# Small norm, gate and softmax operations of a cross-attention and mixture-of-experts kernel, moved from VectorE to other engines

## The chip, the cores and the metric

The kernel runs on one core of a Trainium2 chip. The time is that of one execution on the device, in microseconds (us). Engines: TensorE (PE in the profile), VectorE (DVE), ScalarE (ACT), GpSimd (POOL) and SyncE (SP), which here only issues DMAs.

## The reference

`x` is 8 x 1024 x 1024, `ctx` 8 x 64 x 1024 with a mask of its 64 rows, all float32. Cut to what matters:

```python
xn = layernorm(x)
scores = where(mask, xn @ ctx.T / sqrt(1024), -1e30)
x = x + where(any(mask), softmax(scores) @ ctx, 0)
xn = layernorm(x)
probs = softmax(xn @ router_w.T)                    # 8 experts
w_dense = the two largest of probs, divided by their sum, at their experts; 0 elsewhere
Ax = xn @ lora_A.T                                  # 8 experts x rank 16
x = x + xn @ weight.T + ((Ax * w_dense) @ lora_B) * 2.0
```

## The kernel before

The 8192 rows of x are 64 tiles of 128 rows (one row per partition); eight tiles make a batch element, which has its own ctx and mask. Every engine has its own list of instructions, written out by hand as `step(tile)` for each tile j of a batch; batches 1 to 6 are a hardware loop (`Fori`) on each engine. Semaphores order them: an engine waits with `wait_ge` until a count is reached, and everything behind that wait on the same engine waits too.

To keep float32 accuracy, each large product is done in three passes of split numbers (high and low part): `three` in `base` and `lora_second`, lines L1107 to L1109. The weights stay in SBUF. A `step` of TensorE for tile j has the base product of tile j (xn @ weight, lora_A and router together, in three groups of columns), at odd j the scores of a pair of tiles (L1134), the attention readout of tile j + 2 (L1179, L1180, needs `eT`), and the low-rank second product of tile j.

The path of one tile through the small operations:

- `softmax_scores` (VectorE) makes masked scores and their maximum; `softmax_exp` (ScalarE) exponentiates; `softmax_split` (VectorE) splits e and calls `softmax_sum`, which makes `e_scale` = `any_valid` / sum: a reciprocal (L888) and a product (L890). `e_transposes` turns 32 x 32 blocks, and `e_exchange` on SyncE (L417) moves the blocks in four copies to `e_raw`. ScalarE casts it to `eT` (L590), and the readout can go.
- `add_readout` (VectorE, L897) adds the readout times `e_scale` to x, `norm2_stats` (L903) takes the statistics of the new x, `hT_low` (L973) stands between, and `norm2_moments` makes the mean and variance (L908), `var_eps2` (L910) and `neg_mean2` (L911). Then VectorE goes on with `x2T_low` (L926), two subtractions of 128 x 512 that split the transposed xn of the tile before.
- GpSimd's `norm2` raises `var_eps2` to the power -1/2 (L494) and multiplies it with `neg_mean2` to `shift2` (L497). ScalarE's `norm2` makes `xn` from x with scale and bias (L609).
- `exchange` on SyncE (L381) moves xn to `xq` in four copies, and one step later VectorE turns blocks of it into `x2T` (`x2_transposes`, L919), ScalarE casts the high part (L615), VectorE makes the low part, and TensorE takes the base product.
- `router_top` waits for the router's columns of the base product and finds the two largest (L934 to L939). ScalarE's `gate_exp` makes `gate_num`, the exponential of their difference (L619). `router_gate` makes `gate_den` (L946), its reciprocal `gate_inv` (L949), `gate_b` and `w_dense` (L950, L953), and `h` (L965), which is turned, exchanged and split.

VectorE's order in `step(tile)`, where the change bears: `softmax_split` and `e_transposes` of tile j + 2, `router_top`, `router_gate` and `h_transposes` of tile j, `x2_transposes` of tile j + 1, at odd j `s_transposes` (sum of a pair of scores, L875), `add_readout` and `norm2_stats` of tile j + 2, `hT_low` of tile j, `norm2_moments` of tile j + 2, `x2T_low` of tile j + 1, `softmax_scores` of tile j + 3, then the sums of the output. In steps 3 to 6 the ctx of the next batch is centred and split in addition: `ctx_high` (ScalarE, L542) in step 5 and `ctx_low` (VectorE, L348) in step 6.

SyncE's order in `step(tile)` is `exchange` of xn of tile j + 2 (four copies, first a wait for it), then `e_exchange` of tile j + 3, the store, `h_exchange`, and loads.

For tiles 0 to 2 (and partly 3 and 4) the exchanges are done by TensorE's transposes instead, in orders of their own (`first_norm2` and others).

Of the kernel before, what the change touches and what calls it, by code (L numbers as in the profile page):

```python
# [23 lines left out]
def xattn_lora_moe_kernel(  # L24
# [10 lines left out]
    f32 = mybir.dt.float32  # L35
# [3 lines left out]
    ALU = mybir.AluOpType  # L39
# [69 lines left out]
    with stack:  # L109
# [61 lines left out]
        neg_mean2 = sb("neg_mean2", [P, 1])  # L171
        shift2 = sb("shift2", [P, 1])
# [96 lines left out]
        CONSTANTS = E + 4  # L269
# [37 lines left out]
        neg_mean2_done = sem("neg_mean2_done")  # L307
        shift2_done = sem("shift2_done")
# [164 lines left out]
        def _(pool):  # L473
# [18 lines left out]
            def norm2(tile):  # L492
                pool.wait_ge(ln2_step, count(tile, 4, 4))
# [38 lines left out]
        def _(act):  # L532
# [4 lines left out]
            def ctx_high(b):  # L537
# [4 lines left out]
                act.copy(ctx_hi[:, :], ctx_raw[:, 0:D]).then_inc(ctx_hi_done, 1)  # L542
# [34 lines left out]
            def softmax_exp(tile):  # L577
                act.wait_ge(softmax_step, count(tile, 5, 3))
# [13 lines left out]
            def first_softmax_exp(tile):  # L592
                act.wait_ge(softmax_step, count(tile, 5, 3))
# [166 lines left out]
        def _(dve):  # L760
# [68 lines left out]
            def softmax_scores(tile):  # L829
# [10 lines left out]
                dve.wait_ge(softmax_step, count(tile, 5, 1))  # L840
# [3 lines left out]
                dve.wait_ge(softmax_step, count(tile, 5, 2))  # L844
# [3 lines left out]
            def first_softmax_scores(tile):  # L848
# [542 lines left out]
```

## Time and profile before

| | us |
|---|---|
| median of 3 runs | 999.71 |
| lowest and highest | 997.89, 1001.46 |
| the profiled execution | 1000.15 |
| its span in the trace | 998.2 |
| TensorE matmul busy | 979.6 |
| VectorE busy | 868.6 |
| ScalarE busy | 476.0 |
| GpSimd busy | 144.0 |

The granted clock of TensorE is 1.00 of full speed over the whole span. Busy times are sums over one profiled execution. Matmuls overlap, so that TensorE's busy time doesn't say whether it stands before a given product; the starts of two neighbours do.

### The profile page before, as it was taken

Reading aid. Unit: us, or ns where it says so; the run is one execution under the profiler, and the core shown is the slowest. Engines: PE = TensorE matmul, PEld = TensorE weight load, DVE = VectorE, ACT = ScalarE, POOL = GpSimd, SP = SyncE. Lnnn points to the kernel's source line nnn. Section 1 sums busy time; section 2 is a strip of 40 time slices with the busy share of each in tenths; the row PEclk is TensorE's granted clock in tenths of the full one; section 3 lists DMA queues with packets and bytes.
Section 4 is the critical chain, followed back from the end, with each engine's and each line's share of the span. In section 5 each row is a group of like instructions: output and inputs, shape, how many; then the busy total and the mean of one; then the engine's idle time right before and its main releaser. Section 6 shows DMA issues by size and latency. Waiting matters only on the chain.

```text
span 998.2 us, 18389 instructions
## 1 busy us (share of the span) xinstructions
PE 979.6 (98%) x5849; PEld 950.2 (95%) x5849; DVE 868.6 (87%) x2230; ACT 476.0 (48%) x930; POOL 144.0 (14%) x278
## 2 busy tenths in 40 slices
PE   8999999999999999999999999999999999999998
PEld 7899999999999999999999999999999999999998
DVE  6988988889988899889989899888999889988874
ACT  7755544545444455445455445444454444454420
POOL 3311111111111111111111111111111111111100
PEclk9999999999999999999999999999999999999999
DMA  8555565555566555664555755556565566554432
GB/s 318 180 176 149 150 173 158 160 133 158 165 162 181 148 138 152 172 189 143 138 143 160 208 138 162 130 149 193 158 159 154 128 182 171 156 156 128 112 77 70
DMA packets 156095, 156.61 MB, mean 157 GB/s; under 512 B 93968, under 2 KB 128912, under 8 KB 156048
## 3 DMA queue, kind: packets, MB, share of 16 engines
q1 hardware_dynamic: 155184, 154.63, 56.2%
q10 hardware_dynamic: 864, 1.45, 0.4%
q8 instruction: 18, 0.29, 0.1%
q14 instruction: 29, 0.24, 0.1%
HBM read 78.74 MB, written 33.55 MB: 112 GB/s over the span
## 4 chain that ended last, share of the span: by engine, by line
PE 36%; DVE 22%; DMA 13%; SPq 10%; issue 8%; ACT 5%; POOL 5%; ACTq 0%; POOLq 0%; DVEq 0%
PE base_ps L1107 10%; PE base_ps L1109 10%; PE base_ps L1108 10%; DMA xq<-xn 10%; SPq L381 7%; DVE stats L903 5%; ACT xn L609 4%; DVE x2T L919 4%; DVE w_raw L897 3%; POOL rstd L494 3%; PE s_ps L1134 3%; SPq L417 2%; DMA w_raw<-w_raw 2%; DVE x_first L897 2%; PE ro_ps L1179 1%
## 5 line engine op out<-in xcount | busy, mean ns | idle before, releaser
L1107 PE MATMUL base_ps<-w_hi,xT_hi 128*128 128x392 f32 x1512 | 495.5, 328 | 0.0
L1109 PE MATMUL base_ps<-w_hi,xT_lo 128*128 128x392 f32 x1512 | 494.4, 327 | 0.0
L1108 PE MATMUL base_ps<-w_lo,xT_hi 128*128 128x392 f32 x1512 | 494.4, 327 | 0.0
L1107 PEld LDWEIGHTS base_ps<-w_hi,xT_hi 128*128 128x128 f32 x1512 | 285.9, 189 | 1.7
L1108 PEld LDWEIGHTS base_ps<-w_lo,xT_hi 128*128 128x128 f32 x1512 | 285.8, 189 | 1.6
L1109 PEld LDWEIGHTS base_ps<-w_hi,xT_lo 128*128 128x128 f32 x1512 | 285.8, 189 | 0.0
L919 DVE STREAM_TRANSPOSE x2T<-xq 128x512 f32<-128x512 f32 x122 | 167.2, 1465 | 27.7 <-DMA xq<-xn 27.6
L494 POOL TENSOR_TENSOR rstd<-var_eps,neg_half 128x1 f32<-128x1 f32 x64 | 61.4, 959 | 521.8 <-DVE var_eps L910 521.8
L615 ACT CAST xT_hi<-x2T 128x512 fp32r<-128x512 f32 x122 | 69.5, 616 | 100.9 <-DVE x2T L919 100.9
L590 ACT CAST eT<-w_raw 128x128 fp32r<-128x128 f32 x59 | 17.6, 298 | 166.6 <-DMA w_raw<-w_raw 166.5
L926 DVE TENSOR_TENSOR xT_lo<-x2T,xT_hi 128x512 fp32r<-128x512 f32 x122 | 78.2, 683 | 0.0
L609 ACT ACTIVATE xn<-w_raw,shift,rstd 128x1024 f32<-128x1024 f32 x32 | 39.7, 1241 | 78.6 <-POOL shift L497 78.6
L816 DVE TENSOR_TENSOR xT_parts<-xT_raw,xT_parts 128x1024 fp32r<-128x1024 f32 x62 | 73.4, 1185 | 0.0
L609 ACT ACTIVATE xn<-x_first,shift,rstd 128x1024 f32<-128x1024 f32 x29 | 36.0, 1241 | 71.5 <-POOL shift L497 71.5
L570 ACT CAST xT_parts<-xT_raw 128x1024 fp32r<-128x1024 f32 x64 | 63.8, 1043 | 0.1
L1107 PE MATMUL base_ps<-b_hi,hT_hi 128*128 128x384 f32 (+1 forms) x192 | 60.4, 315 | 1.4 <-DVE hT_lo L973 1.2
L1179 PE MATMUL ro_ps<-ctx_hi,eT 128*128 128x512 f32 x128 | 52.2, 407 | 7.6 <-ACT eT L590 7.0
L1108 PE MATMUL base_ps<-b_lo,hT_hi 128*128 128x384 f32 (+1 forms) x192 | 59.3, 309 | 0.0
L1109 PE MATMUL base_ps<-b_hi,hT_lo 128*128 128x384 f32 (+1 forms) x192 | 59.3, 309 | 0.0
L488 POOL TENSOR_TENSOR var_eps<-sum_sq,eps_sum 128x1 f32<-128x1 f32 x64 | 16.7, 261 | 276.9 <-ACT x2T L561 275.9
L1134 PE MATMUL s_ps<-xT_parts,ctxT 128*128 128x512 f32 x232 | 54.8, 379 | 0.0
L1180 PE MATMUL ro_ps<-ctx_lo,eT 128*128 128x512 f32 x128 | 48.5, 379 | 0.0
(131 smaller groups left out, 1274.2 us busy)
## 6 DMA issues: line engine op xcount, KB each, us to landing
xT_raw<-in_xT SPq DMA_DIRECT2D x62, 512.0 KB, 5.2
xq<-xn SPq DMA_DIRECT2D x244, 128.0 KB, 3.5
w_raw<-in_x SPq DMA_DIRECT2D x32, 512.0 KB, 3.4
out<-x_first SPq DMA_DIRECT2D x32, 512.0 KB, 2.7
out<-w_raw SPq DMA_DIRECT2D x31, 512.0 KB, 2.8
x_first<-in_x SPq DMA_DIRECT2D x30, 512.0 KB, 3.5
h<-w_raw SPq DMA_DIRECT2D x248, 16.0 KB, 2.1
w_raw<-w_raw SPq DMA_DIRECT2D x236, 16.0 KB, 2.6
```

Of the source, the lines that this page charges most:

```text
L381: sp.dma_start(xq[a * QP:(a + 1) * QP, :, :], xn[:, a * DQ:(a + 1) * DQ]).then_inc(xq_loaded, 16)
L494: pool.tensor_tensor(rstd2[:, :], var_eps2[:, :], neg_half[:, :], ALU.pow).then_inc(rstd2_done, 1)
L570: act.copy(xT_hi[:, i], xT_raw[:, k, i]).then_inc(xT_hi_done, 1)
L609: act.activation(xn[:, :], x(tile), ACT.Identity, bias=shift2[:, :], scale=rstd2[:, :]).then_inc(xn_done, 1)
L615: act.copy(chunks(xT2_hi[:, tile[1] % 2], i), chunks(x2T, i)).then_inc(x2T_hi_done, 1)
L816: dve.tensor_tensor(xT_lo[:, i], xT_raw[:, tile[1] // 2 % 2, i], xT_hi[:, i].bitcast(f32), ALU.subtract).then_inc(xT_split, 1)
L919: dve.transpose(out_[:, i * QS:(i + 1) * QS], xq[:, i * QS:(i + 1) * QS, :].rearrange("p g (c n) -> p g c n", n=QP)).then_inc(x2T_done, 1)
L926: dve.tensor_tensor(chunks(xT2_lo[:, k], i), chunks(x2T, i), chunks(xT2_hi[:, k], i).bitcast(f32), ALU.subtract).then_inc(x2T_split, 1)
L1107: pe.matmul(out_, a_hi, w_h, start=start, stop=False, skip_group_check=again)
L1108: pe.matmul(out_, a_hi, w_l, start=False, stop=False, skip_group_check=again)
L1109: return pe.matmul(out_, a_lo, w_h, start=False, stop=stop, skip_group_check=again)
L1134: mm = pe.matmul(s_ps[:, 0:2 * T2], ctxT[:, c, :], xT_parts[:, :, :, c, :].rearrange("p l t n -> p t n l"), start=(c == 0), stop=(c == C - 1))
```

## The change

Four operations on one column (128 x 1) leave VectorE in each tile:

- `var_eps2`, the variance plus epsilon, goes to GpSimd, ahead of its power;
- `neg_mean2` goes to ScalarE, as the first thing of its `norm2`, behind a wait for the mean;
- `gate_den` goes to ScalarE, behind `gate_num`; VectorE now makes `gate_b` ahead of the reciprocal;
- the product of the softmax's inverse sum with `any_valid` goes for tiles from batch 1 on (10 of 64 keep it); instead the ctx of those batches is multiplied with `any_valid` when it is split, in `ctx_high` and `ctx_low`.

Two constants more are set by GpSimd at the start, and the counts of the semaphores follow.

```diff
--- before.py
+++ after.py
@@ -266,7 +268,7 @@
-        CONSTANTS = E + 4
+        CONSTANTS = E + 6
...
@@ -345,8 +350,9 @@
         def ctx_low(engine, b):
             engine.wait_ge(ctx_hi_done, b + 1)
-            engine.tensor_tensor(ctx_lo[:, :], ctx_raw[:, 0:D], ctx_hi[:, :].bitcast(f32),
-                                 ALU.subtract).then_inc(ctx_split, 1)
+            engine.scalar_tensor_tensor(out=ctx_lo[:, :], in0=ctx_raw[:, 0:D], scalar=any_valid[:, :],
+                                        in1=ctx_hi[:, :].bitcast(f32), op0=ALU.mult,
+                                        op1=ALU.subtract).then_inc(ctx_split, 1)
...
@@ -478,6 +484,8 @@
+            pool.memset(eps_mean[:, :], EPS).then_inc(constants_ready, 1)
+            pool.memset(half_one[:, :], 1.0 / SCALING).then_inc(constants_ready, 1)
...
@@ -490,7 +498,9 @@
             def norm2(tile):
-                pool.wait_ge(ln2_step, count(tile, 4, 4))
+                pool.wait_ge(ln2_step, count(tile, 3, 3))
+                pool.tensor_tensor(var_eps2[:, :], mean_var2[:, 1:2], eps_mean[:, :], ALU.add).then_inc(var_eps2_done, 1)
+                pool.wait_ge(var_eps2_done, count(tile, 1, 1))
                 pool.tensor_tensor(rstd2[:, :], var_eps2[:, :], neg_half[:, :], ALU.pow).then_inc(rstd2_done, 1)
                 pool.wait_ge(neg_mean2_done, count(tile, 1, 1))
                 pool.wait_ge(rstd2_done, count(tile, 1, 1))
...
@@ -539,7 +549,11 @@
                 act.wait_ge(readout_done, count((b, 0), 2))
-                act.copy(ctx_hi[:, :], ctx_raw[:, 0:D]).then_inc(ctx_hi_done, 1)
+                if isinstance(b, int) and b == 0:
+                    act.copy(ctx_hi[:, :], ctx_raw[:, 0:D]).then_inc(ctx_hi_done, 1)
+                    return
+                act.wait_ge(mask_step, b * 3 + 3)
+                act.activation(ctx_hi[:, :], ctx_raw[:, 0:D], ACT.Identity, scale=any_valid[:, :]).then_inc(ctx_hi_done, 1)
...
@@ -603,7 +617,13 @@
+            def negative_mean2(tile):
+                act.wait_ge(ln2_step, count(tile, 3, 3))
+                act.wait_ge(shift2_done, count(tile, 1))
+                act.activation(neg_mean2[:, :], mean_var2[:, 0:1], ACT.Identity, scale=-1.0).then_inc(neg_mean2_done, 1)
+
             def norm2(tile):
+                negative_mean2(tile)
                 act.wait_ge(shift2_done, count(tile, 1, 1))
...
@@ -615,9 +635,12 @@
             def gate_exp(tile):
-                act.wait_ge(router_step, count(tile, 7, 1))
+                act.wait_ge(router_step, count(tile, 6, 1))
                 act.activation(gate_num[:, :], top8[:, 0:1], ACT.Exp, bias=top8[:, 1:2],
                                scale=-1.0).then_inc(gate_exp_done, 1)
+                act.wait_ge(gate_exp_done, count(tile, 1, 1))
+                act.activation(gate_den[:, :], gate_num[:, :], ACT.Identity, bias=half_one[:, :],
+                               scale=1.0 / SCALING).then_inc(gate_den_done, 1)
...
@@ -885,12 +909,16 @@
             def softmax_sum(tile):
-                dve.reciprocal(e_inv[:, :], e_sum[:, :]).then_inc(softmax_step, 1)
-                dve.wait_ge(softmax_step, count(tile, 5, 4))
+
+                if tile[0] > 0:
+                    dve.reciprocal(e_scale[:, :], e_sum[:, :]).then_inc(softmax_step, 1)
+                    return
+                dve.reciprocal(e_inv[:, :], e_sum[:, :]).then_inc(e_inv_done, 1)
+                dve.wait_ge(e_inv_done, count(tile, 1, 1))
                 dve.tensor_tensor(e_scale[:, :], e_inv[:, :], any_valid[:, :], ALU.mult).then_inc(softmax_step, 1)
...
@@ -903,12 +931,9 @@
             def norm2_moments(tile):
-                dve.wait_ge(ln2_step, count(tile, 4, 2))
+                dve.wait_ge(ln2_step, count(tile, 3, 2))
                 dve.sem_inc(waits_alone, 1)
                 dve.bn_aggr(mean_var2[:, :], stats2[:, :]).then_inc(ln2_step, 1)
-                dve.wait_ge(ln2_step, count(tile, 4, 3))
-                dve.tensor_scalar(var_eps2[:, :], mean_var2[:, 1:2], EPS, None, ALU.add).then_inc(ln2_step, 1)
-                dve.tensor_scalar(neg_mean2[:, :], mean_var2[:, 0:1], -1.0, None, ALU.mult).then_inc(neg_mean2_done, 1)
...
@@ -943,16 +968,15 @@
                 dve.wait_ge(gate_exp_done, count(tile, 1, 1))
-                dve.tensor_scalar(gate_den[:, :], gate_num[:, :], 1.0, 1.0 / SCALING, ALU.add, ALU.mult)\
-                   .then_inc(router_step, 1)
-                dve.wait_ge(router_step, count(tile, 7, 4))
-                dve.reciprocal(gate_inv[:, :], gate_den[:, :]).then_inc(router_step, 1)
+                dve.wait_ge(router_step, count(tile, 6, 3))
                 dve.tensor_scalar(gate_b[:, :], iota8[:, :], top2_at[:, 1:2], gate_num[:, :], ALU.is_equal, ALU.mult)\
                    .then_inc(router_step, 1)
-                dve.wait_ge(router_step, count(tile, 7, 6))
+                dve.wait_ge(gate_den_done, count(tile, 1, 1))
+                dve.reciprocal(gate_inv[:, :], gate_den[:, :]).then_inc(router_step, 1)
+                dve.wait_ge(router_step, count(tile, 6, 4))
                 dve.scalar_tensor_tensor(out=w_dense[:, :], in0=iota8[:, :], scalar=top2_at[:, 0:1], in1=gate_b[:, :],
                                          op0=ALU.is_equal, op1=ALU.add).then_inc(router_step, 1)
...
```

## Rows read from the trace of the kernel before

**Rows 1.** The page, part 1 (busy) and part 4 (the chain that ended last).

```profile
...
PE 979.6 (98%) x5849; PEld 950.2 (95%) x5849; DVE 868.6 (87%) x2230; ACT 476.0 (48%) x930; POOL 144.0 (14%) x278
...
PE base_ps L1107 10%; PE base_ps L1109 10%; PE base_ps L1108 10%; DMA xq<-xn 10%; SPq L381 7%; DVE stats L903 5%; ACT xn L609 4%; DVE x2T L919 4%; DVE w_raw L897 3%; POOL rstd L494 3%; PE s_ps L1134 3%; SPq L417 2%; DMA w_raw<-w_raw 2%; DVE x_first L897 2%; PE ro_ps L1179 1%
...
```

**Rows 2.** The waits: engine, line, releaser, us in total, times, longest.

```profile
...
DVE x2T L919 <- DMA xq<-xn: 27.6, 42, 2.8
...
PE ro_ps L1179 <- ACT eT L590: 7.0, 16, 1.4
...
```

**Rows 3.** The timeline of step 1 of batch 4: start, us, engine, line; in brackets idle before.

```profile
...
544.26 0.21 DVE L908 BATCH_NORM_AGGREGATE mean_var<-stats 128x2 f32<-128x12 f32 x1
...
544.50 0.15 DVE L910 TENSOR_SCALAR var_eps<-mean_var 128x1 f32<-128x1 f32 x1
...
544.58 0.14 DVE L911 TENSOR_SCALAR neg_mean<-mean_var 128x1 f32<-128x1 f32 x1
544.64 1.28 DVE L926 TENSOR_TENSOR xT_lo<-x2T,xT_hi 128x512 fp32r<-128x512 f32 x2
...
544.74 0.99 POOL L494 TENSOR_TENSOR rstd<-var_eps,neg_half 128x1 f32<-128x1 f32 x1 [9.37 <-DVE var_eps L910]
...
545.87 0.30 POOL L497 TENSOR_TENSOR shift<-neg_mean,rstd 128x1 f32<-128x1 f32 x1
...
546.20 1.24 ACT L609 ACTIVATE xn<-x_first,shift,rstd 128x1024 f32<-128x1024 f32 x1 [2.58 <-POOL shift L497]
...
```

**Rows 4.** The timeline after it, to the next step's readout.

```profile
...
547.47 2.54 SPq L381 DMA_DIRECT2D xq<-xn  x4
...
550.06 2.55 SPq L417 DMA_DIRECT2D w_raw<-w_raw  x4
...
553.05 2.68 DVE L919 STREAM_TRANSPOSE x2T<-xq 128x512 f32<-128x512 f32 x2 [0.34 <-DMA xq<-xn]
...
553.76 0.33 PE L1108 MATMUL base_ps<-w_lo,xT_hi 128*128 128x384 f32 x1
...
553.91 0.30 ACT L590 CAST eT<-w_raw 128x128 fp32r<-128x128 f32 x1 [2.90 <-DMA w_raw<-w_raw]
553.93 0.33 PE L1109 MATMUL base_ps<-w_hi,xT_lo 128*128 128x384 f32 x1
...
554.26 0.48 PE L1179 MATMUL ro_ps<-ctx_hi,eT 128*128 128x512 f32 x1
...
```

**Rows 5.** GpSimd's power by its line: ns, shortest, median, longest.

```profile
...
L494 POOL TENSOR_TENSOR rstd<-var_eps,neg_half x64: 547/986/990, 18.1 to 966.7; 128x1 f32<-128x1 f32 x64
...
```

**Rows 6.** The timeline: GpSimd's sum and power inside ctx_low, and in the free.

```profile
...
489.91 1.22 DVE L348 TENSOR_TENSOR ctx_lo<-ctx_raw,ctx_hi 128x1024 fp32r<-128x1024 f32 x1
...
490.53 0.65 POOL L488 TENSOR_TENSOR var_eps<-sum_sq,eps_sum 128x1 f32<-128x1 f32 x1 [4.24 <-ACT x2T L561]
...
550.40 0.19 POOL L488 TENSOR_TENSOR var_eps<-sum_sq,eps_sum 128x1 f32<-128x1 f32 x1 [4.24 <-ACT x2T L561]
...
550.67 0.55 POOL L490 TENSOR_TENSOR rstd<-var_eps,neg_half 128x1 f32<-128x1 f32 x1
...
```

**Rows 7.** The timeline of xn (a step 5), reduction (step 1), shift (step 3).

```profile
...
365.41 1.24 ACT L609 ACTIVATE xn<-w_raw,shift,rstd 128x1024 f32<-128x1024 f32 x1 [1.01 <-POOL shift L497]
...
540.34 0.69 DVE L875 TENSOR_REDUCE w_raw<-s_ps 128x256 f32<-128x512 f32 x1 [0.24 <-PE s_ps L1134]
...
576.66 0.19 POOL L497 TENSOR_TENSOR shift<-neg_mean,rstd 128x1 f32<-128x1 f32 x1
...
```

**Rows 8.** Groups by line: count, busy us, mean ns, idle before.

```profile
...
L926 DVE TENSOR_TENSOR xT_lo<-x2T,xT_hi 128x512 fp32r<-128x512 f32 x122 | 78.2, 683 | 0.0
...
L542 ACT CAST ctx_hi<-ctx_raw 128x1024 fp32r<-128x1024 f32 x8 | 8.3, 1043 | 0.0
...
```

**Rows 9.** The timeline of the head, tiles 1 and 2 on ScalarE.

```profile
...
47.68 0.29 ACT L619 ACTIVATE gate_num<-top 128x1 f32<-128x1 f32 x1 [1.60 <-DVE top L934]
...
48.03 1.52 ACT L644 ACTIVATE xn<-x_first,shift,rstd 128x512 f32<-128x512 f32 x2
...
```

More of the change, by code:

```diff
@@ L171, in xattn_lora_moe_kernel @@
         neg_mean2 = sb("neg_mean2", [P, 1])
+        eps_mean = sb("eps_mean", [P, 1])
+        half_one = sb("half_one", [P, 1])
         shift2 = sb("shift2", [P, 1])
@@ L307, in xattn_lora_moe_kernel @@
         neg_mean2_done = sem("neg_mean2_done")
+        var_eps2_done = sem("var_eps2_done")
+        gate_den_done = sem("gate_den_done")
+        e_inv_done = sem("e_inv_done")
         shift2_done = sem("shift2_done")
@@ L577, in softmax_exp @@
             def softmax_exp(tile):
-                act.wait_ge(softmax_step, count(tile, 5, 3))
+                act.wait_ge(softmax_step, count(tile, 4, 3))
                 if turned_on_pe(tile, 6):
@@ L592, in first_softmax_exp @@
             def first_softmax_exp(tile):
-                act.wait_ge(softmax_step, count(tile, 5, 3))
+                act.wait_ge(softmax_step, count(tile, 4, 3))
                 act.wait_ge(e_split_done, count(tile, 1))
@@ L639, in first_norm2 @@
             def first_norm2(tile):
+                negative_mean2(tile)
                 act.wait_ge(shift2_done, count(tile, 1, 1))
@@ L839, in softmax_scores @@
                    .then_inc(softmax_step, 1)
-                dve.wait_ge(softmax_step, count(tile, 5, 1))
+                dve.wait_ge(softmax_step, count(tile, 4, 1))
                 dve.scalar_tensor_tensor(out=by_blocks(s_all[:, :]), in0=s_raw[:, 0:2, k, :], scalar=rstd1[:, :],
@@ L843, in softmax_scores @@
                    .then_inc(softmax_step, 1)
-                dve.wait_ge(softmax_step, count(tile, 5, 2))
+                dve.wait_ge(softmax_step, count(tile, 4, 2))
                 dve.tensor_reduce(out=neg_max[:, :], in_=s_all[:, :], axis=AX.X, op=ALU.max,
@@ L855, in first_softmax_scores @@
                                          in1=mask_bias[:, :], op0=ALU.mult, op1=ALU.add).then_inc(softmax_step, 1)
-                dve.wait_ge(softmax_step, count(tile, 5, 1))
+                dve.wait_ge(softmax_step, count(tile, 4, 1))
                 dve.scalar_tensor_tensor(out=s_all[:, :], in0=st_ps[:, 0:M], scalar=rstd1[:, :],
                                          in1=s_part[:, :], op0=ALU.mult, op1=ALU.add).then_inc(softmax_step, 1)
-                dve.wait_ge(softmax_step, count(tile, 5, 2))
+                dve.wait_ge(softmax_step, count(tile, 4, 2))
                 dve.tensor_reduce(out=neg_max[:, :], in_=s_all[:, :], axis=AX.X, op=ALU.max,
@@ L887, in softmax_sum @@
             def softmax_sum(tile):
-                dve.reciprocal(e_inv[:, :], e_sum[:, :]).then_inc(softmax_step, 1)
-                dve.wait_ge(softmax_step, count(tile, 5, 4))
+                if tile[0] > 0:
[3 more added lines that the diff above has]
+                dve.wait_ge(e_inv_done, count(tile, 1, 1))
                 dve.tensor_tensor(e_scale[:, :], e_inv[:, :], any_valid[:, :], ALU.mult).then_inc(softmax_step, 1)
             def add_readout(tile):
-                dve.wait_ge(softmax_step, count(tile, 5, 5))
+                dve.wait_ge(softmax_step, count(tile, 4, 4))
                 for i in range(2):
@@ L934, in router_top @@
                 dve.max(top8[:, :], logits).then_inc(router_step, 1)
-                dve.wait_ge(router_step, count(tile, 7, 1))
+                dve.wait_ge(router_step, count(tile, 6, 1))
                 dve.sem_inc(waits_alone, 1)
                 dve.max_index(top8_at[:, :], top8[:, :], logits).then_inc(router_step, 1)
-                dve.wait_ge(router_step, count(tile, 7, 2))
+                dve.wait_ge(router_step, count(tile, 6, 2))
                 dve.tensor_copy(top2_at[:, :], top8_at[:, 0:2]).then_inc(router_step, 1)
```

2 lines of the change are left out of this document (1 added, 1 removed).

## The prediction

> **What bounds the kernel.** I read the page's first part, the waits, and then one pair of tiles in the timeline. The first part gives TensorE 98% of the span and VectorE 87% [rows 1], so VectorE looks like a good place to save. The chain that ended last says something narrower: beside the matmuls it runs through the exchange of xn (10% in its transfer, 7% in SyncE's issuing), the norm2 statistics, ScalarE's xn and GpSimd's power [rows 1]. In the waits [rows 2], TensorE stands before its readout for eT (16 visible waits), and VectorE stands before its transposes of x2T, 42 times, for the exchange of xn. Nobody waits for the four small operations themselves.
>
> Rows 3 and 4 show why. Call a VectorE `step` by j, its tile's place in its batch of eight. In step 1 of batch 4, bn_aggr starts at 544.26, var_eps at 544.50, the power at 544.74, the shift at 545.87, xn at 546.20 [rows 3]. SyncE then issues four copies of xn (547.47 to 550.01), and only then four copies of e for the next readout, 550.06 to 552.61, since they stand behind the others in its queue. The eT cast starts at 553.91 and the readout at 554.26; the matmul before it started at 553.93, 0.33 earlier, where the one before that had come 0.17 earlier [rows 4]. So TensorE lost 0.16 there, to a chain that began with bn_aggr. xn to eT is 7.71 us. The same xn also feeds the transposes at 553.05, 6.85 us after it, for which VectorE had waited 0.34 [rows 4]; these lead to the next bn_aggr. Two loops thus pass through "bn_aggr to xn": one through TensorE every second tile, one through the exchange every tile. Both run at the pace of the kernel. **What counts is how late xn comes after bn_aggr, and not how much VectorE has to do.**
>
> **The change, part by part.**
>
> *Moving var_eps to GpSimd.* Before, with bn_aggr's end (544.47) as zero: var_eps ends at +0.18, the power starts at +0.27, ends at +1.26, shift ends at +1.70, xn starts at +1.73 [rows 3]. The power took 0.99 here, 0.986 in the median, but 0.547 at its shortest [rows 5]. It began 0.10 after VectorE's x2T subtraction, which has both inputs in SBUF, and 544.74 + 0.99 - 0.547 = 545.18 is where it really got going: 0.54 after the subtraction's start at 544.64. So a GpSimd operation behind such a subtraction is held for about the first 0.54 us of its 0.68 [rows 8]. The very kind of operation that is added, a 128x1 sum on GpSimd, shows it as well: 0.65 instead of 0.19 when it starts inside ctx_low's subtraction [rows 6].
>
> After, VectorE has nothing between bn_aggr and the x2T subtractions. The first can follow with the overlap of 0.07 to 0.08 that rows 3 show between neighbours: -0.08. GpSimd hears of bn_aggr 0.09 after its end, as the power heard of var_eps (544.65 to 544.74). So the new sum starts at +0.09, behind the subtraction, is held to -0.08 + 0.54 = +0.46 and ends at +0.65 (0.19 free). The power follows 0.08 later, the gap of 550.40 + 0.19 to 550.67 [rows 6], at +0.73. The second subtraction has begun at +0.52 (0.60 after the first, from 1.28 for the two less 0.68) and holds it to +1.06; it ends at +1.61. Shift starts 0.14 later (+1.75) as before, takes 0.19, xn starts at about +1.97. Call the delay d = 1.97 - 1.73 = **+0.24 us a tile**. The bounds: if the new sum slips in before the subtraction takes hold, it ends at +0.28, the power waits for the first subtraction only (to +0.46), ends at +1.01, and xn starts at +1.37: d = -0.36. If the first subtraction starts no sooner than var_eps did (+0.03), all of it comes 0.11 later: d = +0.35. The nearest row, a sum held by a subtraction, is the middle case, and I take it.
>
> The Trainium skill (SBUF — State Buffer, section "Who interferes with whom") says that a VectorE instruction with two SBUF inputs contends with a GpSimd one that reads SBUF, and that the later one is blocked for the whole instruction. The trace agrees on who is held, and shows the hold ending 0.54 us into an instruction of 0.68. By the page's full length xn would start at about +2.1: an estimate of d = +0.38, and of 1013 us.
>
> *neg_mean on ScalarE.* About 0.30 for one column, as gate_num [rows 9], needed only when the power ends (+1.61). ScalarE stood idle 2.58 before xn at [rows 3] and 1.01 in the tightest kind of step, the fifth [rows 7], so it is free by +0.72 there, +0.92 with the slower ctx cast, and done by +1.3. Hidden, by the power. Where the cover is gone it costs 0.30 plus shift: at the head, below.
>
> *gate_den on ScalarE, with gate_b ahead of the reciprocal.* VectorE drops 0.15, as var_eps [rows 3]; the reciprocal now needs gate_num plus another 0.30. So the gate ends between 0.15 earlier and 0.15 later. Both lie before the transposes' wait of 0.34 for the exchange [rows 4] and are worth nothing there; were that wait gone, up to 0.15 a tile.
>
> *e_scale folded into ctx.* 54 of 64 one-column products, also of about 0.15, go. e gets turned 0.2 earlier and then stands behind SyncE's copies of xn just the same [rows 4]: nothing. The ctx cast becomes an activation with a vector scale, 1.24 as xn [rows 3] for 1.04 [rows 8], seven times, ahead of two casts in step 5 where ScalarE had 1.01 left. ctx_low becomes scalar_tensor_tensor on the same inputs: I take the same 1.22 [rows 6]; bounds are no change and a second pass of 1.22, seven times, in step 6, where the transposes wait next to nothing.
>
> VectorE loses some 0.6 us a tile in all. That matters only in steps 4 and 6, which VectorE enters late because of ctx work.
>
> **The sum over a batch.** I follow how late each xn gets; slack is where another partner was last. Step 1: the pair sum of the scores waited 0.24 for TensorE [rows 7], so its start is set by TensorE, which is late by what the previous eT was: from step 7 over step 0 to step 1 only one d gets through. Step 2, by the exchange: d. Step 3: d + 0.11, since there the shift took 0.19 before too, not 0.30 [rows 3, 7]. Step 4's readout follows that xn by eT. Step 5's reduction is set by VectorE, with TensorE some 0.2 to 0.3 ahead (an estimate from the 0.24 of step 1): -0.3, and + d. Step 6 hands this on to TensorE by eT, and step 7 adds d. A batch of eight tiles gets 5d - 0.2 = **1.0 us** later. From tile 8 to tile 61 that is 54/8 = 6.75 batches: 6.8 us. The rest of batch 0 has three of these steps after its slower start: 0.5.
>
> *The head.* For the first tiles GpSimd isn't held, but ScalarE comes to xn without time to spare. For tile 2 gate_num ends at 47.97 and xn starts at 48.03 [rows 9]. Now gate_den (0.33) and neg_mean (0.30) stand in front, then the shift (0.06 + 0.19) and 0.03: 48.9, or 48.7 as gate_num comes 0.2 earlier; +0.65. TensorE waits for this tile's split right after. Tiles 0 and 1 get some 0.2 and 0.15 by the same count. Head: +1.0.
>
> Sum: 6.8 + 0.5 + 1.0 = 8.3 us on a profiled execution of 1000.15 (span 998.2 and 2 around it). That execution lies 0.4 above the median of 999.71, so I say **1008 us**, 0.8% slower.
>
> **The rivals.** (a) *The sum slips past the subtraction* (d = -0.36): xn comes earlier, TensorE can then only regain what it loses before readouts, 7.0 us in visible waits [rows 2] plus some of the small ones; with DMA-late steps staying, 4 to 5 us: 995, faster. It decides if VectorE's subtraction starts later than +0.09. Against it: the power already came behind one at +0.10 with an instruction more ahead of it. 8%. (b) *VectorE's relief wins*: if steps 4 and 6 set the pace, 0.5 us in two steps a batch, 14 to 15 steps, with half of it regained: 3 to 4 us, 996. For it: 87% busy; against: 42 waits for the exchange. 7%. (c) *Covered*: TensorE is the bound and the loops have slack, the change moves idle time only: 1000. Against: the readouts follow eT directly. 9%. (d) *Held to the subtraction's end, or a later start.* With the full 0.68 for each hold, the sum ends at -0.08 + 0.68 + 0.19 = +0.79, the power at +0.52 + 0.68 + 0.55 = +1.75, and xn starts 0.36 later, d = 0.38; with the later start d = 0.35: six d a batch less 0.5 of slack, 1.6 to 1.8 for the 1.0, so 4 to 5 us more: 1012 to 1013. 16%. The forecast: 60%.
>
> **Numbers.** A measurement of this kernel can tell about 0.3% (3 us) from nothing. Slower: 0.60 + 0.16 and little more: 0.77. Within: 0.10. Faster: 0.13. The range reaches from 1001.5, half-covered delays, to 1013.5, case (d): it leaves out (a), (b) and part of (c).
>
> **What the profile after would show.** The new sum (var_eps from mean_var on GpSimd) at a median near 0.56 and not 0.19, the power near 0.88, and xn 1.9 to 2.0 after bn_aggr; the visible waits of TensorE for eT up from 7 us to 13 or more; VectorE's busy time down by some 35 us and its idle before the transposes up; ScalarE's neg_mean before the power's end in all but the first four tiles. I'm wrong if the new sum takes 0.19, if xn comes no later, or if waits for eT don't grow although it does.

## The result, and the profile after

The changed kernel takes 1005.08 us (median of 5 runs, 1003.50 to 1005.45) against 999.42 for the kernel before (5 runs): 5.7 us slower, ratio 1.0054 with a 95% interval of 1.0038 to 1.0069. The profiled execution is its fastest, 1003.50 us with a span of 1001.6. A second measurement, beside the last two experiments, gave 1.0048 (1.0035 to 1.0061). The forecast was 1008, in a range of 1001.5 to 1013.5.

The page of the changed kernel, part 1 and part 4:

```profile
...
PE 978.5 (98%) x5849; PEld 950.0 (95%) x5849; DVE 841.6 (84%) x1984; ACT 505.4 (50%) x1058; POOL 161.8 (16%) x344
...
SPq L387 10%; DMA xq<-xn 10%; PE base_ps L1131 7%; PE base_ps L1132 7%; PE base_ps L1133 7%; DVE stats L931 6%; ACT xn L629 6%; POOL rstd L504 4%; SPq L423 4%; DVE x2T L944 4%; DMA w_raw<-w_raw 4%; DVE w_raw L925 3%; DVE x_first L925 3%; POOL var_eps L502 2%; PE s_ps L1158 2%
...
```

VectorE is relieved as meant: 27 us less than in [rows 1], while ScalarE has 29 and GpSimd 18 more. But the chain that ended last now has less of the matmuls (7% each for 10%) and more of SyncE's issuing of xn (10% for 7%), and GpSimd's new sum (L502) appears in it.

The timeline of the same step as [rows 3], in the changed kernel:

```profile
...
545.14 0.21 DVE L936 BATCH_NORM_AGGREGATE mean_var<-stats 128x2 f32<-128x12 f32 x1
545.27 1.24 DVE L951 TENSOR_TENSOR xT_lo<-x2T,xT_hi 128x512 fp32r<-128x512 f32 x2
...
545.39 0.20 ACT L623 ACTIVATE neg_mean<-mean_var 128x1 f32<-128x1 f32 x1 [0.62 <-DVE mean_var L936]
545.43 0.52 POOL L502 TENSOR_TENSOR var_eps<-mean_var,eps_mean 128x1 f32<-128x1 f32 x1 [9.03 <-DVE mean_var L936]
...
546.03 0.88 POOL L504 TENSOR_TENSOR rstd<-var_eps,neg_half 128x1 f32<-128x1 f32 x1
...
547.06 0.19 POOL L507 TENSOR_TENSOR shift<-neg_mean,rstd 128x1 f32<-128x1 f32 x1
...
547.28 1.24 ACT L629 ACTIVATE xn<-x_first,shift,rstd 128x1024 f32<-128x1024 f32 x1 [1.69 <-POOL shift L507]
...
```

bn_aggr ends at 545.35. VectorE's subtraction starts 0.08 before that end, GpSimd's sum 0.08 after it. It takes 0.52 where such a sum takes 0.19 in the free [rows 6], and the power behind it 0.88 for 0.55: each is held by one of the two subtractions. xn starts 1.93 us after bn_aggr's end, for 1.73 in [rows 3]. neg_mean on ScalarE is done at 545.59, long before the power. What follows, to the next readout:

```profile
...
548.55 2.54 SPq L387 DMA_DIRECT2D xq<-xn  x4
...
554.81 0.33 PE L1133 MATMUL base_ps<-w_hi,xT_lo 128*128 128x384 f32 x1
555.01 0.30 ACT L604 CAST eT<-w_raw 128x128 fp32r<-128x128 f32 x1 [2.80 <-DMA w_raw<-w_raw]
...
555.36 0.48 PE L1203 MATMUL ro_ps<-ctx_hi,eT 128*128 128x512 f32 x1 [0.23 <-ACT eT L604]
...
```

xn to eT is 7.73 us (7.71 before), so nothing in between has changed; the readout comes 0.55 after the matmul before it, for 0.33 in [rows 4]. That is 0.22 more, the 0.20 by which xn is late after bn_aggr. GpSimd's sum and power over all tiles (ns: shortest, median, longest), and the waits:

```profile
...
L502 POOL TENSOR_TENSOR var_eps<-mean_var,eps_mean x64: 189/523/527, 18.0 to 970.5; 128x1 f32<-128x1 f32 x64
...
```

```profile
...
L504 POOL TENSOR_TENSOR rstd<-var_eps,neg_half x64: 548/882/887, 18.3 to 971.1; 128x1 f32<-128x1 f32 x64
...
```

```profile
...
DVE x2T L944 <- DMA xq<-xn: 35.1, 48, 2.4
...
PE ro_ps L1203 <- ACT eT L604: 11.8, 30, 1.3
...
```

TensorE now visibly waits for eT 30 times and 11.8 us, for 16 times and 7.0 us in [rows 2], and VectorE waits for the exchange 35.1 us for 27.6. By the starts of neighbouring matmuls it is plainer: summed over the profiled execution, the time from the matmul before to each matmul of L1203 (L1179 before) grew by 4.2 us, where the span grew by 3.4. A second profiled execution of the changed kernel gives 5.2 and 5.2. So TensorE lost its time before the readouts.

### The profile page after: what moved, and what is told of

Its sections match the earlier page's. It is cut to its first block, busy times and chain, and to the rows that moved or that the text cites. A ratio compares the mean times of both kernels' runs of the same rounds, so it can differ in the third digit from the quotient of the medians.

```text
span 1001.6 us, 18525 instructions
## 1 busy us (share of the span) xinstructions
PE 978.5 (98%) x5849; PEld 950.0 (95%) x5849; DVE 841.6 (84%) x1984; ACT 505.4 (50%) x1058; POOL 161.8 (16%) x344
## 4 chain that ended last, share of the span: by engine, by line
PE 26%; DVE 21%; DMA 15%; SPq 15%; issue 8%; POOL 8%; ACT 7%; ACTq 0%; POOLq 0%; DVEq 0%
SPq L387 10%; DMA xq<-xn 10%; PE base_ps L1131 7%; PE base_ps L1132 7%; PE base_ps L1133 7%; DVE stats L931 6%; ACT xn L629 6%; POOL rstd L504 4%; SPq L423 4%; DVE x2T L944 4%; DMA w_raw<-w_raw 4%; DVE w_raw L925 3%; DVE x_first L925 3%; POOL var_eps L502 2%; PE s_ps L1158 2%
## 5 line engine op out<-in xcount | busy, mean ns | idle before, releaser
L944 DVE STREAM_TRANSPOSE x2T<-xq 128x512 f32<-128x512 f32 x122 | 165.5, 1451 | 35.6 <-DMA xq<-xn 35.1
L502 POOL TENSOR_TENSOR var_eps<-mean_var,eps_mean 128x1 f32<-128x1 f32 x64 | 32.2, 503 | 507.0 <-DVE mean_var L936 507.0
L951 DVE TENSOR_TENSOR xT_lo<-x2T,xT_hi 128x512 fp32r<-128x512 f32 x122 | 75.6, 662 | 0.0
L1203 PE MATMUL ro_ps<-ctx_hi,eT 128*128 128x512 f32 x128 | 52.2, 408 | 11.9 <-ACT eT L604 11.8
L504 POOL TENSOR_TENSOR rstd<-var_eps,neg_half 128x1 f32<-128x1 f32 x64 | 55.1, 862 | 5.0
```

The lines of the kernel that those rows point to most:

```text
L504: pool.tensor_tensor(rstd2[:, :], var_eps2[:, :], neg_half[:, :], ALU.pow).then_inc(rstd2_done, 1)
L944: dve.transpose(out_[:, i * QS:(i + 1) * QS], xq[:, i * QS:(i + 1) * QS, :].rearrange("p g (c n) -> p g c n", n=QP)).then_inc(x2T_done, 1)
L951: dve.tensor_tensor(chunks(xT2_lo[:, k], i), chunks(x2T, i), chunks(xT2_hi[:, k], i).bitcast(f32), ALU.subtract).then_inc(x2T_split, 1)
```

## The experiments

Each was timed beside the kernel before. "xn after bn_aggr" is the start of xn (L609 in the kernel before) less the end of bn_aggr, in a regular step of the profiled execution.

### var_eps back on VectorE

```diff
 # the changed kernel, with
-                pool.wait_ge(ln2_step, count(tile, 3, 3))
-                pool.tensor_tensor(var_eps2[:, :], mean_var2[:, 1:2], eps_mean[:, :], ALU.add).then_inc(var_eps2_done, 1)
                 pool.wait_ge(var_eps2_done, count(tile, 1, 1))
...
                 dve.bn_aggr(mean_var2[:, :], stats2[:, :]).then_inc(ln2_step, 1)
+                dve.wait_ge(ln2_step, count(tile, 3, 3))
+                dve.tensor_scalar(var_eps2[:, :], mean_var2[:, 1:2], EPS, None, ALU.add).then_inc(var_eps2_done, 1)
```

> The changed kernel with var_eps alone back on VectorE, ahead of the x2T subtractions. Theory (how late xn comes after bn_aggr sets the time): the power starts behind the first subtraction once, not the sum and the power behind one each; xn 1.55 to 1.65 us after bn_aggr's end (before 1.73, after 1.93), so 995 to 999 us. Rival (what costs is the work given to ScalarE, or the ctx split with the mask): all of that is still here, so 1003 us or more.

Measured: 999.02 us, ratio 0.9989 (0.9979 to 0.9998); xn 1.67 after bn_aggr. The whole loss went with this one operation, and ScalarE's two operations, the new ctx split and the gate stayed. The time was at the top of what was expected. The rival is out.

### VectorE waits until GpSimd's sum is done

```diff
 # the changed kernel, with
                     norm2_moments(nxt2)
+                    dve.wait_ge(var_eps2_done, count(nxt2, 1, 1))
                 if exists(nxt):
                     x2T_low(nxt)
```

> The changed kernel, with VectorE waiting for GpSimd's sum before its x2T subtractions in the regular steps. The sum should take 0.19 and not 0.52, the power be held by the first subtraction only, and xn start about 1.82 after bn_aggr (after 1.93). VectorE idles 0.4 us a tile more. Theory (the delay of xn): 1001 to 1004 us, below the changed kernel's 1005. Rival (VectorE's load sets the pace): slower than the changed kernel, 1007 or more.

Measured: 1004.02 us, ratio 1.0042 (1.0028 to 1.0055). The timeline of one step:

```profile
...
545.48 0.21 DVE L936 BATCH_NORM_AGGREGATE mean_var<-stats 128x2 f32<-128x12 f32 x1
...
545.77 0.19 POOL L502 TENSOR_TENSOR var_eps<-mean_var,eps_mean 128x1 f32<-128x1 f32 x1 [9.42 <-DVE mean_var L936]
...
546.00 1.29 DVE L951 TENSOR_TENSOR xT_lo<-x2T,xT_hi 128x512 fp32r<-128x512 f32 x2 [0.30 <-POOL var_eps L502]
546.04 1.06 POOL L504 TENSOR_TENSOR rstd<-var_eps,neg_half 128x1 f32<-128x1 f32 x1
...
547.57 1.24 ACT L629 ACTIVATE xn<-x_first,shift,rstd 128x1024 f32<-128x1024 f32 x1 [1.64 <-POOL shift L507]
...
```

The sum takes 0.19 now and is done before the subtraction at 546.00, which holds the power alone. xn starts 1.88 after bn_aggr's end (545.69), and the time lies below the changed kernel's ratio of 1.0054 and 1.0048, in the direction of the delay (the power, which starts 0.04 behind the subtraction, is held longer than expected, and xn came at 1.88 and not 1.82), although VectorE stands idle for 0.3 us more in each step. The intervals overlap, so by itself this says only that VectorE's idle time cost nothing.

### var_eps alone moved

```diff
 # the kernel before, with
             def norm2(tile):
-                pool.wait_ge(ln2_step, count(tile, 4, 4))
+                pool.wait_ge(ln2_step, count(tile, 3, 3))
+                pool.tensor_tensor(var_eps2[:, :], mean_var2[:, 1:2], eps_mean[:, :], ALU.add).then_inc(var_eps2_done, 1)
+                pool.wait_ge(var_eps2_done, count(tile, 1, 1))
...
                 dve.wait_ge(ln2_step, count(tile, 3, 3))
-                dve.tensor_scalar(var_eps2[:, :], mean_var2[:, 1:2], EPS, None, ALU.add).then_inc(ln2_step, 1)
                 dve.tensor_scalar(neg_mean2[:, :], mean_var2[:, 0:1], -1.0, None, ALU.mult).then_inc(neg_mean2_done, 1)
```

> The kernel before with var_eps alone moved to GpSimd; neg_mean stays on VectorE between bn_aggr and the subtractions, so that GpSimd's sum and VectorE's first subtraction start within 0.02 us of each other. Theory: if the sum is first it takes 0.19, xn comes 1.6 after bn_aggr and the time is 997 to 1000; if it is held it takes 0.6 or more, xn comes 2.1 or later and the time is 1007 or more; the recorded durations and the time must go together. Rival (only VectorE's load counts): 998 to 1000 whichever it is.

Measured: 997.90 us, ratio 0.9978 (0.9968 to 0.9988). The sum takes 0.191 us (median), the power 0.870, and xn comes 1.59 after bn_aggr. So moving var_eps to GpSimd is a gain of 2 us as long as neg_mean stays behind on VectorE, and a loss of 5.7 when neg_mean goes too.

### The gate and the ctx edits alone

```diff
 # the changed kernel, with var_eps2 and neg_mean2 back on VectorE
                 dve.bn_aggr(mean_var2[:, :], stats2[:, :]).then_inc(ln2_step, 1)
+                dve.wait_ge(ln2_step, count(tile, 3, 3))
+                dve.tensor_scalar(var_eps2[:, :], mean_var2[:, 1:2], EPS, None, ALU.add).then_inc(var_eps2_done, 1)
+                dve.tensor_scalar(neg_mean2[:, :], mean_var2[:, 0:1], -1.0, None, ALU.mult).then_inc(neg_mean2_done, 1)
```

> The kernel before with the gate's and the softmax's edits (gate_den on ScalarE, e_scale folded into the ctx split), while var_eps and neg_mean stay on VectorE. Theory: xn stays at 1.73 after bn_aggr; VectorE's relief is worth something in the steps with ctx work only: 996 to 999.5. Rival (these edits are what costs): 1002 or more.

Measured: 999.40 us, ratio 0.9991 (0.9982 to 1.0000), xn 1.73 after bn_aggr. VectorE is busy 857 us for 869, and the kernel gains at most 1 to 2 us from it.

### hT_low behind the moments, in the changed kernel and in the one before

```diff
 # both, each on its own kernel
-                hT_low(tile)
                 if exists(nxt2):
                     norm2_moments(nxt2)
+                hT_low(tile)
                 if exists(nxt):
                     x2T_low(nxt)
```

> The changed kernel with hT_low put behind norm2_moments. bn_aggr comes 0.23 earlier, and what follows it is a short subtraction (128 columns), so that GpSimd's sum slips in ahead of the long ones: the sum 0.19, xn 1.5 to 1.6 after bn_aggr, 0.4 earlier in all than before the change. Theory (the delay of xn, and TensorE as the floor): the whole loss goes, 996 to 999 us. Rival (the work given to ScalarE or the ctx edits cost as well): some of the loss stays, 1001 or more.

> The kernel before with hT_low put behind norm2_moments, all else as it was. xn 1.6 after bn_aggr and bn_aggr 0.23 earlier. Theory: as the shorter delays of var_eps alone gave 2 us, some 2 to 4 us faster than before, 996 to 998. Rival (TensorE is the floor already): within 1 us of before.

Measured: on the changed kernel 1009.79 us, ratio 1.0104 (1.0087 to 1.0121), xn 2.13 after bn_aggr; on the kernel before 1005.23 us, 1.0057 (1.0045 to 1.0069), xn 1.73. The theory missed both times. The first time lies in the rival's open range (1001 or more), but not for the rival's reason: the delay grew, and the work on ScalarE is the same. On the changed kernel GpSimd's sum came too late again, as the timeline shows:

```profile
...
548.74 0.21 DVE L936 BATCH_NORM_AGGREGATE mean_var<-stats 128x2 f32<-128x12 f32 x1
548.87 0.24 DVE L997 TENSOR_TENSOR hT_lo<-h,hT_hi 128x128 fp32r<-128x128 f32 x1
...
549.02 1.28 DVE L951 TENSOR_TENSOR xT_lo<-x2T,xT_hi 128x512 fp32r<-128x512 f32 x2
549.03 0.72 POOL L502 TENSOR_TENSOR var_eps<-mean_var,eps_mean 128x1 f32<-128x1 f32 x1 [8.99 <-DVE mean_var L936]
...
```

The subtraction (L951) starts at 549.02, the sum at 549.03 and takes 0.72. hT_low's short subtraction, which also has two inputs in SBUF, had started ahead of both, so this row alone doesn't say how close the race with L951 was. Other rows help: in one tile where the sum started 0.04 behind hT_low's subtraction and that one was recorded with 0.29, it was held for 0.11 only, until 0.14 before the end of that subtraction; by that measure hT_low had let go before 549.02.

On the kernel before, GpSimd's shift came behind the second subtraction of L926 (from 546.45 on):

```profile
...
545.75 0.59 POOL L494 TENSOR_TENSOR rstd<-var_eps,neg_half 128x1 f32<-128x1 f32 x1 [9.38 <-DVE var_eps L910]
545.85 1.28 DVE L926 TENSOR_TENSOR xT_lo<-x2T,xT_hi 128x512 fp32r<-128x512 f32 x2
...
546.48 0.70 POOL L497 TENSOR_TENSOR shift<-neg_mean,rstd 128x1 f32<-128x1 f32 x1
...
```

The power is nearly free now, but the shift takes 0.70 for 0.30 in [rows 3], so xn starts 1.73 after bn_aggr as before and not 1.6. And another product had to wait. TensorE's waits:

```profile
...
PE base_ps L1107 <- DVE hT_lo L973: 6.6, 13, 1.0
...
PE ro_ps L1179 <- ACT eT L590: 0.5, 3, 0.2
...
```

TensorE hardly waits for eT any more (0.5 us, for 7.0 in [rows 2]), but 6.6 us before the low-rank product, for hT_lo, which was nearly free of waits as long as hT_low stood in front of the moments. By the starts of neighbouring matmuls, TensorE regained 10.4 us before the readouts and lost 14.7 at the first two matmuls of the low-rank groups (L1107, L1108), against a span 4.1 longer. The swap moved the wait from one product to the other, and made it longer. I had priced hT_low's own 0.23 us and not asked who waits for it.

### One more GpSimd sum before the power

```diff
 # the kernel before, with
+                pool.tensor_tensor(var_again2[:, :], var_eps2[:, :], zero[:, :], ALU.add).then_inc(var_again2_done, 1)
+                pool.wait_ge(var_again2_done, count(tile, 1, 1))
-                pool.tensor_tensor(rstd2[:, :], var_eps2[:, :], neg_half[:, :], ALU.pow).then_inc(rstd2_done, 1)
+                pool.tensor_tensor(rstd2[:, :], var_again2[:, :], neg_half[:, :], ALU.pow).then_inc(rstd2_done, 1)
```

> The kernel before with one more sum on GpSimd (plus zero) between var_eps and the power, everything else as it was: VectorE, ScalarE and the ctx split untouched. The suspected cost by itself, doubled: the new sum held by the first subtraction, the power by the second, xn 2.2 after bn_aggr, d about 0.47. Theory: at 28 us of time for each us of d (what the changed kernel and the one that waits for the sum gave) 13 us slower, 1011 to 1015. Rival (the loss of the change came from its other parts, or GpSimd's delay is mostly covered): under 1005.

Measured: 1018.09 us, ratio 1.0183 (1.0166 to 1.0199), 18.6 us more. The timeline of one step and TensorE's wait:

```profile
...
551.50 0.21 DVE L914 BATCH_NORM_AGGREGATE mean_var<-stats 128x2 f32<-128x12 f32 x1
...
551.88 1.28 DVE L932 TENSOR_TENSOR xT_lo<-x2T,xT_hi 128x512 fp32r<-128x512 f32 x2
...
551.98 0.63 POOL L498 TENSOR_TENSOR var_again<-var_eps,zero 128x1 f32<-128x1 f32 x1 [9.12 <-DVE var_eps L916]
...
552.69 0.88 POOL L500 TENSOR_TENSOR rstd<-var_again,neg_half 128x1 f32<-128x1 f32 x1
...
553.94 1.24 ACT L615 ACTIVATE xn<-x_first,shift,rstd 128x1024 f32<-128x1024 f32 x1 [2.85 <-POOL shift L503]
...
```

```profile
...
PE ro_ps L1185 <- ACT eT L596: 22.9, 31, 1.7
...
```

The added sum starts 0.10 after the subtraction and takes 0.63, the power is held again, xn starts 2.23 after bn_aggr's end (551.71): 0.50 more than before. VectorE, ScalarE and the ctx split are those of the kernel before. By the starts of its matmuls, TensorE lost 15.5 us before the readouts, where the span grew by 15.9. So the suspected cost alone makes a loss, and a larger one than I expected: 37 us of time for each us of delay, where the changed kernel has 5.1 to 5.7 for 0.20, or 25 to 28.

### The copies of e issued by ScalarE

```diff
 # the kernel before, with e_exchange taken from SyncE and put into ScalarE's step
                 if exists(after(tile, 3)):
                     norm1_mean(after(tile, 3))
+                if exists(nxt2) and not turned_on_pe(nxt2, 5):
+                    e_exchange(nxt2)      # act.wait_ge(eq_done, ...), act.wait_ge(eT_copied, ...), four act.dma_start
+                if exists(after(tile, 3)):
                     norm1_squares(after(tile, 3))
                 gate_exp(tile)
```

> The kernel before with the four copies of e issued from ScalarE's queue (between its two norm1 passes) and not from SyncE's behind the copies of xn. It takes the xn chain out of the way to eT. Theory: eT comes 2 us earlier, TensorE's visible waits for eT (7 us) mostly go, and the time is 994 to 997 us. Rival: issuing holds ScalarE 2.5 us a tile, its casts of x2T or its xn come late and the time is the same or longer, 1000 to 1006.

Measured: 1079.42 us, ratio 1.0791 (1.0773 to 1.0809). Both theories missed, the rival in size. ScalarE's timeline of one step, and the waits:

```profile
...
557.59 0.56 ACTq L583 DMA_DIRECT2D w_raw<-w_raw  x1
...
558.18 2.51 ACTq L583 DMA_DIRECT2D w_raw<-w_raw  x3
560.80 1.15 ACT L553 ACTIVATE x2T<-x_first,neg_mean 128x1024 f32<-128x1024 f32 x1 [3.02 <-issue]
...
```

```profile
...
ACT x2T L553 <- issue: 159.4, 58, 3.9
...
DVE gate_den L947 <- ACT gate_num L617: 122.7, 59, 3.2
...
PE ro_ps L1180 <- ACT eT L588: 56.5, 38, 3.4
...
```

Issuing four copies takes ScalarE's queue 3.1 us (557.59 to 560.69), the norm1 squares and with them gate_num come that much later, and VectorE stands before gate_den for 122.7 us, which delays all else in its queue, the turned e of the next tile included. The test doesn't tell what eT without xn's copies ahead would be worth.

### neg_mean alone back on VectorE, and an operation without a use

```diff
 # the first: the changed kernel without negative_mean2 on ScalarE, and with
                 dve.bn_aggr(mean_var2[:, :], stats2[:, :]).then_inc(ln2_step, 1)
+                dve.wait_ge(ln2_step, count(tile, 3, 3))
+                dve.tensor_scalar(neg_mean2[:, :], mean_var2[:, 0:1], -1.0, None, ALU.mult).then_inc(neg_mean2_done, 1)
...
 # the second: the changed kernel, neg_mean2 still on ScalarE, and with
+                dve.wait_ge(ln2_step, count(tile, 3, 3))
+                dve.tensor_scalar(unused2[:, :], mean_var2[:, 0:1], -1.0, None, ALU.mult).then_inc(unused2_done, 1)
```

> The changed kernel with neg_mean alone back on VectorE, between bn_aggr and the subtractions; var_eps stays on GpSimd, the gate and ctx edits stay. Theory: neg_mean keeps the subtraction back by 0.18, so GpSimd's sum comes first and takes 0.19, xn 1.6 after bn_aggr: 995.5 to 998.5 us, at least as fast as var_eps moved alone. Rival (the cost of the change lies in the sum's move itself or in the rest of the edits): 1002 to 1005.

> The changed kernel plus one one-column operation on VectorE after bn_aggr whose output nobody reads; ScalarE goes on making neg_mean. Pure added work of 0.15 us a tile for VectorE. Theory (who takes hold of SBUF first): faster than the changed kernel by 5 us or more, 996 to 999. Rival (VectorE's load, or ScalarE's neg_mean, costs the time): 1005 or more.

> The changed kernel once more, beside the two above on one chip. All theories: 1004 to 1006 us; xn 1.93 after bn_aggr.

Measured, the three beside each other: neg_mean back 996.97 us, ratio 0.9968 (0.9957 to 0.9979); the operation without a use 997.10 us, 0.9981 (0.9972 to 0.9991); the changed kernel once more 1004.74 us, 1.0048 (1.0035 to 1.0061), with xn 1.93 after bn_aggr. One step of the kernel with the unused operation:

```profile
...
542.49 0.21 DVE L938 BATCH_NORM_AGGREGATE mean_var<-stats 128x2 f32<-128x12 f32 x1
...
542.74 0.15 DVE L940 TENSOR_SCALAR unused<-mean_var 128x1 f32<-128x1 f32 x1
542.78 0.19 POOL L504 TENSOR_TENSOR var_eps<-mean_var,eps_mean 128x1 f32<-128x1 f32 x1 [9.18 <-DVE mean_var L938]
...
542.81 1.30 DVE L955 TENSOR_TENSOR xT_lo<-x2T,xT_hi 128x512 fp32r<-128x512 f32 x2
...
543.05 0.87 POOL L506 TENSOR_TENSOR rstd<-var_eps,neg_half 128x1 f32<-128x1 f32 x1
...
544.29 1.24 ACT L631 ACTIVATE xn<-x_first,shift,rstd 128x1024 f32<-128x1024 f32 x1 [1.35 <-POOL shift L509]
...
```

The unused operation starts at 542.74. The subtraction behind it starts at 542.81 and not before bn_aggr's end (542.70), and GpSimd's sum starts at 542.78, 0.03 before it. That is all the difference: the sum takes 0.19, the power is held once, xn starts 1.59 after bn_aggr. **Adding 0.15 us of work to VectorE in each tile made the changed kernel 7 to 8 us faster.** The first kernel of this pair does the same with an operation that is of use, and is the fastest by its median, 2.6 us under the kernel before; its interval overlaps those of the unused operation and of var_eps moved alone.

Side by side, by the delay:

| kernel | xn after bn_aggr, us | ratio to before |
|---|---|---|
| changed, neg_mean back | 1.58 | 0.9968 |
| before, var_eps alone moved | 1.59 | 0.9978 |
| changed, with an unused operation | 1.59 | 0.9981 |
| changed, var_eps back | 1.67 | 0.9989 |
| before, gate and ctx edits | 1.73 | 0.9991 |
| before | 1.73 | 1 |
| changed, VectorE waits for the sum | 1.88 | 1.0042 |
| changed | 1.93 | 1.0054, 1.0048 |
| before, one more sum | 2.23 | 1.0183 |

## Why the prediction was right

**What bounds the kernel.** Shown. The time follows how late xn comes after bn_aggr through the nine kernels of the table, with VectorE 84% to 87% busy in all of them (the two swaps stand apart, since another wait takes part there); taking work from VectorE without touching that delay gained about 1 us at most, and adding work that shortened it gained 7 to 8. Where TensorE loses the time is shown by its starts: before the readouts, for 4.2 to 5.2 us in the changed kernel and 15.5 with one more sum.

**Who is held, and for how long.** Shown. The sum was expected near 0.56 and the power near 0.88; they took 0.523 and 0.882. The hold ended before the subtraction did: 545.43 + 0.52 - 0.19 = 545.76, 0.49 after the subtraction's start and not the 0.54 that I took from the kernel before. The reason is in the rows: the subtraction that starts before bn_aggr's end is recorded with 0.64 and not 0.68 (the pair takes 1.24 for 1.28), and in both kernels the hold ends 0.14 before the recorded end. The prediction read the hold as the first 0.54 us; its own [rows 6] show that the length of the instruction sets it: behind ctx_low's 1.22 the sum got going 1.08 after the start, 0.14 before the end again. The Trainium skill (SBUF — State Buffer, "Who interferes with whom") says that issue order decides who is blocked: the trace agrees for starts that lie clearly apart, with the sum at 0.19 when it started 0.03 ahead of the subtraction and at 0.52 when it started 0.16 behind. Its full-length hold, by which xn would have come about 2.1 after bn_aggr, isn't what this kernel shows. xn came at 1.93 and not 1.97: d was 0.20 for 0.24, since the second subtraction starts 0.04 earlier too.

The order of the recorded starts has an edge: in the head of the kernel with one more sum, a shift that is recorded 0.01 ahead of a long subtraction was held all the same.

```profile
...
31.52 1.27 POOL L503 TENSOR_TENSOR shift<-neg_mean,rstd 128x1 f32<-128x1 f32 x1
...
31.53 2.35 DVE L822 TENSOR_TENSOR xT_parts<-xT_raw,xT_parts 128x1024 fp32r<-128x1024 f32 x2
...
```

So 0.01 ahead was not enough, and 0.03 ahead was, in every regular tile of the three kernels in which the sum slipped in.

**neg_mean.** Its own time was hidden, as forecast, and 0.20 and not 0.30. But the prediction counted its leaving VectorE only as part of "VectorE has nothing between" the two and never priced the edit apart. It is the edit that decides: with neg_mean on VectorE the moved var_eps gains about 2 us. I gave the case in which the sum slips in an 8% chance for the change as it stands, and it didn't happen, but I didn't see that one of the edits was what closed it. The price of that case was also too high on one side: with xn at +1.59, not +1.37, it was worth 2 to 3 us and not 4 to 5. I had let the subtraction start at -0.08 in that case; where the sum wins, it starts at +0.11 (542.81), and holds the power to 0.56 after that.

**The sum over a batch** is the term that was too large. Readouts of the first tiles of batches 1 and 7, of the kernel before:

```profile
...
129.41 0.45 PE L1179 MATMUL ro_ps<-ctx_hi,eT 128*128 128x512 f32 x1 [0.86 <-ACT eT L590]
...
857.89 0.48 PE L1179 MATMUL ro_ps<-ctx_hi,eT 128*128 128x512 f32 x1
...
```

and of the changed kernel, with that of tile 4 ahead of them:

```profile
...
67.26 0.38 PE L1203 MATMUL ro_ps<-ctx_hi,eT 128*128 128x512 f32 x1
...
129.13 0.45 PE L1203 MATMUL ro_ps<-ctx_hi,eT 128*128 128x512 f32 x1 [0.68 <-ACT eT L604]
...
860.85 0.48 PE L1203 MATMUL ro_ps<-ctx_hi,eT 128*128 128x512 f32 x1 [0.17 <-ACT eT L604]
...
```

Over these six batches the changed kernel lost (860.85 - 129.13) - (857.89 - 129.41) = 3.2 us, or 0.54 a batch; its second profiled execution gives 0.65 by the same two readouts. The prediction had 1.0. The smaller d accounts for 5 x 0.04 = 0.2 of what is missing.

The rest sits in steps 3 and 4. With d at 0.20 the prediction's terms let the readouts get later by 0.20 in step 0, 0.20 in step 2, 0.51 in step 4 and -0.10 in step 6; averaged over the six batches they got later by 0.20, 0.33, -0.09 and 0.09 (in the second execution 0.21, 0.43, -0.08 and 0.09). So the term that was mis-sized is what steps 2 and 3 hand on to the readout of step 4: nothing for 0.51. From batch to batch that term scatters between -0.8 and +1.3 in a single execution, and why its mean is nothing stays open. The sum also had no term for xn of step 4, which came 0.10 *sooner* after bn_aggr than before: in the kernel before, the shift there stood behind a subtraction of the ctx work (L788, from 590.85; the shift took 0.70 from 590.88), and in the changed kernel, where it comes later, it takes 0.29.

The transfers differ as well: from issue to landing, the last copy of xn in the step with the ctx loads took 4.7 to 5.7 us in the changed kernel and 4.9 to 6.2 in the one before, for a median of 3.5 over all copies. The steeper slope with the doubled sum (37 against 25 to 28 us for each us of delay) fits slack that is used up first, and the 5d of eight steps (5/8 of 59 tiles is 37); this was argued, not tested.

**The head** was wrong: +1.0 was forecast, and at the readout of tile 4 the profiled execution of the changed kernel is at 67.26, that of the one before at 67.70, so 0.4 earlier. ScalarE's rows for tile 2, to be held against [rows 9]:

```profile
...
47.62 0.29 ACT L642 ACTIVATE gate_den<-gate_num,half_one 128x1 f32<-128x1 f32 x1
...
47.83 0.18 ACT L623 ACTIVATE neg_mean<-mean_var 128x1 f32<-128x1 f32 x1
...
48.34 1.53 ACT L668 ACTIVATE xn<-x_first,shift,rstd 128x512 f32<-128x512 f32 x2 [0.33 <-POOL shift L507]
...
```

neg_mean took 0.18 and not 0.30, and gate_den starts at 47.62, 0.06 before gate_num did in [rows 9], so that xn is late by 0.31 (48.34 for 48.03) and not by 0.65. VectorE's relief in the head, which the sum left out, is the likely reason for the rest. The readout of tile 4 comes at 66.8 to 67.3 in the three profiled executions in which VectorE has nothing left behind bn_aggr (the changed kernel twice, and the one that waits for the sum in its regular steps), and at 67.6 to 67.7 in the three where one operation is left there (var_eps back, neg_mean back, the unused one). The kernel with the gate and ctx edits alone, with both operations left, is at 67.5, so single executions settle this only roughly.

The profiled executions differ by 3.4 us in their spans (the second one of the changed kernel by 5.2), the medians by 5.7: the single executions scatter by 2 us, so these terms are good to that. The direction and its mechanism were right, the size was too large (8.3 for 5.7) by the batch term and by the head.

**The other edits.** gate_den and e_scale were worth nearly nothing, as forecast. The ctx cast became 1.15 us for 1.04, and ctx_low 1.28 for 1.22, seven times each. VectorE's busy time fell by 27 us and not by 35, and the visible waits for eT rose to 11.8 us (12.7 in the second execution) and not to 13 or more; the other signs came as listed.

## What to carry to other kernels

When a small operation moves to GpSimd, look at what VectorE does in the tenth of a microsecond in which GpSimd learns of its input: if a VectorE instruction with two inputs in SBUF starts first, GpSimd waits for most of its length, whatever its own work is. Taking the small operation out from in front of that instruction can be what makes it start first, so edits that are harmless one by one need to be priced together. And relief of an engine that is 87% busy is worth little (here about 1 us in 1000) if its waits are for a loop through other engines' queues; the length of that loop is what to count.

## What the runs showed of the hardware

- An order of start that differs by hundredths of a microsecond decides over 0.33 to 0.53 us of a GpSimd operation: its sum took 0.19 when recorded 0.03 ahead of VectorE's subtraction, 0.52 when 0.16 behind, 0.72 when 0.01 behind. One recorded 0.01 ahead was still held.
- The hold ended 0.14 us before the recorded end of the subtraction, for recorded lengths of 0.29, 0.64, 0.68 and 1.22 us.
- GpSimd got its turn between two back-to-back subtractions in every regular tile (power at 0.88 with 0.55 of its own), and the second subtraction didn't get longer for it.
- ScalarE's one-column operation is 0.20 us with constants for scale and bias (neg_mean), and 0.295 with a bias from SBUF (gate_den).
- Four small copies issued from ScalarE's queue kept it 3.1 us, and the kernel lost 79 us.

For those who go on: the best version here is the changed kernel with neg_mean left on VectorE, 0.32% under the kernel before.
